# Later weights split into high and low parts by converting and adding GpSimd transfers, with new order lists

## The reference, cut to what matters

```
h0  = concat(cls_tok, patches @ W_tok.T)
x   = bi_wkv(ln(h0) @ Wk.T, ln(h0) @ Wv.T) * sigmoid(ln(h0) @ Wr.T) @ Wo.T   # scans over 37 rows
h1  = ... + sigmoid(xn @ Wr_f.T) * (relu(xn @ Wk_f.T)**2 @ Wv_f.T)            # channel mix
c   = top-4 of sigmoid(h1n @ router.T) within the 2 best of 4 groups, scaled
out = h1 + sum_e c_e * (silu(h1n @ gWg[e].T) * (h1n @ gWu[e].T)) @ gWd[e] + shared expert
```

## Time and profile before

| | |
|---|---|
| median of 3 runs | 259.08 us (258.5 to 260.05) |
| the profiled execution | 259.53 us, span 257.6 us |
| PE busy | 245.2 us, 95% |
| DVE busy | 191.2 us, 74% |
| ACT busy | 151.5 us, 59% |
| POOL busy | 17.1 us, 7% |
| PE clock granted, mean | 0.996 of full speed |

### The profile page before, as it was taken

One profiled execution on the slowest core, in us unless ns is written; L12 is line 12 of the kernel. 1 busy time (PEld: TensorE's weight loads), 2 busy tenths in 40 slices (PEclk: granted clock), 3 DMA queues, 4 the chain that ended last, 5 costly groups with the idle time before them and its releaser, 6 DMA issues.

```text
span 257.6 us, 4492 instructions
## 1 busy us (share of the span) xinstructions
PE 245.2 (95%) x1508; PEld 222.6 (86%) x1508; DVE 191.2 (74%) x491; ACT 151.5 (59%) x312; POOL 17.1 (7%) x26
## 2 busy tenths in 40 slices
PE   6988879999999998999999999999999999999994
PEld 4866458578588898999999999999999999999993
DVE  4459988999989998999797799887333175853542
ACT  2399798988868998853795971426441432132220
POOL 5100202003101000101100000101000010000000
PEclk9999999999999999999999999999999999999998
DMA  5668563000000342000003520000144000015500
GB/s 154 211 191 286 212 186 119 0 3 0 0 0 6 84 111 57 0 3 0 1 3 121 187 76 4 1 3 0 54 163 158 29 3 0 1 23 109 102 29 26
DMA packets 13015, 17.49 MB, mean 68 GB/s; under 512 B 2336, under 2 KB 11074, under 8 KB 12866
## 3 DMA queue, kind: packets, MB, share of 16 engines
q1 hardware_dynamic: 12722, 17.11, 22.3%
q10 hardware_dynamic: 272, 0.11, 0.2%
HBM read 16.22 MB, written 0.99 MB: 67 GB/s over the span
## 4 chain that ended last, share of the span: by engine, by line
PE 74%; DVE 9%; ACT 9%; issue 3%; DMA 2%; POOL 0%; SPq 0%; DVEq 0%; POOLq 0%; ACTq 0%
PE PG L964 18%; PE PA L984 17%; PE PG L966 11%; PE PF L984 7%; PE PQ L964 4%; PE PQ L966 3%; PE PX L1001 2%; PE PF L1001 2%; ACT norm L417 2%; DMA w_tok<-in_w_tok 2%; PE PF L974 1%; PE PG L1119 1%; PE PG L1118 1%; DVE K L763 1%; PE PF L991 1%
## 5 line engine op out<-in xcount | busy, mean ns | idle before, releaser
L575 ACT ACTIVATE act<-PG,columns 128x222 f32<-128x222 f32 (+3 forms) x56 | 28.4, 507 | 59.0 <-PE PG L966 45.9
L964 PE MATMUL PG<-stack,hi_egu 128*128 128x222 f32 (+1 forms) x288 | 62.2, 324 | 0.0
L913 DVE SCALAR_TENSOR_TENSOR hid<-PG,columns,act 128x222 f32<-128x222 f32 (+1 forms) x52 | 27.3, 524 | 29.3 <-PE PG L966 26.7
L984 PE MATMUL PA<-w_ed,hid 128*124 128x192 f32 (+1 forms) x240 | 46.1, 327 | 0.6 <-DVE hid L922 0.5
L964 PEld LDWEIGHTS PG<-stack,hi_egu 128*128 128x128 f32 x288 | 45.7, 191 | 0.9 <-DVE hid L913 0.4
L966 PE MATMUL PG<-stack,lo_egu 128*128 128x222 f32 (+1 forms) x192 | 42.8, 304 | 0.0
L984 PEld LDWEIGHTS PA<-w_ed,hid 128*124 128x124 f32 (+1 forms) x240 | 38.6, 183 | 1.3 <-issue 1.3
L966 PEld LDWEIGHTS PG<-stack,lo_egu 128*128 128x128 f32 x192 | 31.8, 191 | 0.0
L391 POOL TENSOR_TENSOR rstd<-var,minus_half 112x2 f32<-112x2 f32 (+3 forms) x12 | 13.8, 1146 | 191.7 <-DVE var L657 191.7
L922 DVE TENSOR_TENSOR hid<-hid,gates 128x222 f32<-128x222 f32 (+1 forms) x48 | 21.9, 461 | 1.6 <-DMA gates<-c_rows 0.7
L984 PE MATMUL PF<-w_down,mix_hid 128*124 128x192 f32 (+1 forms) x120 | 22.8, 326 | 0.0
(11 more groups left out here) (248 smaller groups left out, 441.3 us busy)
## 6 DMA issues: line engine op xcount, KB each, us to landing
gates<-in_w_egu SPq DMA_DIRECT2D x6, 512.0 KB, 4.9
gates<-c_rows SPq DMA_DIRECT2D x16, 138.8 KB, 2.9
gates<-c_rows SPq DMA_DIRECT2D x16, 92.5 KB, 2.7
gates<-c_rows SPq DMA_DIRECT2D x16, 83.2 KB, 2.5
w_ed<-in_w_ed SPq DMA_DIRECT2D x1, 1152.0 KB, 6.1
gates<-c_rows SPq DMA_DIRECT2D x16, 55.5 KB, 2.5
gates<-in_w_up SPq DMA_DIRECT2D x2, 384.0 KB, 4.5
pat<-in_patches SPq DMA_DIRECT2D x2, 370.0 KB, 4.3
```

The lines of the kernel that those rows point to most:

```text
L575: nc.scalar.activation(act[128 - gate:128, n % 2, 0:G.n], PG[0:gate, gate_bank(n), 0:G.n], ACT.Silu, bias=bias).then_inc(act_silu, 1)
L913: V_.scalar_tensor_tensor(out, PG[part, 1, 0:G.n], bias, act[part, i, 0:G.n], ALU.add, ALU.mult).then_inc(mul_done, 1)
L964: mm(out, w_hi[:, slot, cols], x[:, p, 0:G.n], start=(p == 0), stop=False, skip_group_check=True)
L984: last = mm(tile_out(P, G, t), src[:, G.ts[t]:G.ts[t] + G.tp], w, start=start and t != 1, stop=stop, skip_group_check=True)
```

## The change

`rf`, `up0`, `up1`, `sgu` and `egu0` to `egu5` no longer go through the ring. POOL starts a transfer from DRAM straight into `hi` that converts to fp32r (`W:` steps of POOL). ACT writes minus the high part into `lo` (`L:` steps of ACT), and POOL starts a second transfer of the same weight that adds the fp32 value onto `lo` (`L:` steps of POOL). PE waits for that second transfer. The low-part matmuls of PE, the copies of ACT at L409 and L400 for these weights and the subtractions of DVE for `rf`, `up` and `sgu` are gone. `router` moves ahead in the ring, and SP's list gets shorter. The exponents' subtractions on PE now use PSUM tile PA instead of PQ, PX and PG, with the waits changed to suit. All four order lists are new; POOL's list now has 12 roots and 20 transfers.

```diff
+            def pool_casts(pool):
+                for name, _ in CAST:
+                    nc.gpsimd.dma_start(hi[name][:, :, :], A[f"w_{name}"]).then_inc(cast_in[name], 16)
+                    yield name
+
+            def pool_lows(pool):
+                for n, (name, _) in enumerate(CAST):
+                    pool.wait_ge(act_minus, n + 1)
+                    nc.gpsimd.dma_start(lo[name][:, :, :], A[f"w_{name}"], accum_op=ALU.add).then_inc(low_in[name], 16)
+                    yield name
...
-        def act_low_parts(act_e):
-
-            for i, (name, _, _, cols, _) in enumerate(PIECES[FIRST_EGU:]):
-                for s in range(2):
-                    act_e.wait_ge(pe_low, 2 * i + s + 1)
-                    nc.scalar.activation(lo[name][:, s, :], PA[:, s, 0:cols], ACT.Copy).then_inc(act_low, 1)
-                    yield f"{name}{'ab'[s]}"
+        def act_minus_parts(act_e):
+
+            for name, _ in CAST:
+                act_e.wait_ge(cast_in[name], 16)
+                nc.scalar.activation(lo[name][:, :, :], hi[name][:, :, :].bitcast(F32), ACT.Copy, scale=-1.0).then_inc(act_minus, 1)
+                yield name
...
         def need(pe, name):
-            split(pe, PIECE_AT[name] + 1)
+            if name in low_in:
+                pe.wait_ge(low_in[name], 16)
+            else:
+                pe.wait_ge(lo_done, PIECE_AT[name] + 1)
...
-        def pe_low_parts(pe):
...
         def sub_bank(g, i):
-            return PG[:, :, :].rearrange("p b c -> p (b c)") if g else (PQ, PX)[i % 2]
+            return PA[:, :, :].rearrange("p b c -> p (b c)") if g else PA[:, i % 2, :]
...
-POOL_ORDER = [(1, 0), (1, 1), (2, 0), (1, 2), (3, 0), (2, 1), (1, 3), (3, 1), (2, 2), (3, 2), (2, 3), (3, 3)]
+POOL_ORDER = _order(
+    "R0:root1 R1:root1 W:rf W:up0 W:up1 W:sgu L:rf L:up0 W:egu0 W:egu1 W:egu2 W:egu3 W:egu4 L:up1 L:sgu R0:root2 R2:root1",
+    "W:egu5 R0:root3 L:egu0 L:egu1 L:egu2 R1:root2 L:egu3 L:egu4 L:egu5 R3:root1 R1:root3 R2:root2 R2:root3 R3:root2",
+    "R3:root3",
+)
 PE_ORDER = _order(
...
+    "H:early0 H:early1 H:early2 H:early3 F0:tok0 H:early4 H:early5 H:tok H:stats0 H:stats1 H:aggr F0:tr1a F0:tr1b F1:tok0",
+    "F1:tok1 F0:k F0:kt F0:v F0:rt F0:r H:var H:rstd H:scan0 F0:sub0 F0:sub1 F0:sub2 F1:tr1a F1:tr1b F2:tok0 H:scan1 F1:k",
+    "F1:kt H:sb0 F0:o0 F1:v F1:rt F1:r F2:tok1 H:sb1 H:e1 H:edge M0:tr2 F1:sub0 F1:sub1 F1:sub2 M0:rf M0:up0 M0:up1 M0:mix0",
+    "M0:up2 M0:mix1 M0:up3 F2:tr1a M0:mix2 M0:up4 M0:mix3 F2:tr1b M0:up5 M0:mix4 M0:mix5 F1:o0 F1:o1 M0:tr3 F2:k G0:g0",
+    "M0:logits G0:g1 F2:kt G0:v1 G0:g2 M1:tr2 G0:v2 G0:g3 F2:v D0:cT D0:d1 G0:v3 G0:g4 D0:d0 F2:rt G0:v4 G0:g5 F2:r M1:rf",
...
 ACT_ORDER = _order(
...
+    "W:cls W:mask W:k F0:tok0 W:v W:r F0:ln1 F0:tr1a F0:tr1b Z0:x0 F1:tok0 F1:tok1 F0:k F0:kt F0:vt F0:kf F0:v F0:rt F0:r",
+    "F0:exps F0:expe F1:ln1 W:router F0:w0 F0:w1 F0:w2 F0:wr F1:tr1a F1:tr1b L:rf L:up0 F1:k F1:kt F1:vt F1:kf L:up1 F1:v",
+    "L:sgu L:egu0 F2:tok0 F1:rt F1:r F1:exps F2:tok1 M0:ln2 Z1:x0 F1:expe F1:w0 M0:tr2 F1:w1 F2:ln1 F1:w2 F1:wr M0:rf",
+    "M0:mix0 M0:mix1 M0:mix2 M0:mix3 F2:tr1a M0:mix4 M0:mix5 L:egu1 F2:tr1b L:egu2 L:egu3 M0:ln3 M0:tr3 Y0:e0 F2:k",
...
+    "M1:mix0 F2:expe M1:mix1 F2:w0 F2:w1 F2:w2 F2:wr M1:mix2 Y0:e6 M1:mix3 Z2:x0 F3:tok0 Y0:e7 L:egu5 Y0:e8 M1:mix4 F3:ln1",
...
 DVE_ORDER = _order(
...
+    "W:cls W:mask F0:stats1 F0:aggr1 F0:var1 F0:ln1 W:k W:v W:r F0:tr1a F0:tr1b F1:stats1 F1:aggr1 F0:scan0 F0:scan1",
+    "F1:var1 F0:sb F0:e1 F0:edge F0:top0 F0:top1 F0:sa F1:ln1 F0:ab00 F0:ab01 F0:ab10 F0:ab11 F0:weigh0 F0:weigh1 F0:own",
+    "F0:sum F1:tr1a F0:sum2 F1:tr1b F0:den F0:recip0 F0:recip1 W:router F0:z F1:scan0 F0:x10 F0:x1 F1:scan1 M0:stats2",
+    "M0:aggr2 F1:sb M0:var2 F1:e1 M0:ln2 F1:edge F1:top0 F1:top1 F1:sa F2:stats1 F2:aggr1 F1:ab00 F2:var1 F1:ab01 F1:ab10",
+    "F2:ln1 F1:ab11 M0:tr2a M0:tr2b F1:weigh0 F1:weigh1 F1:own F1:sum F1:sum2 F1:den F1:recip0 F1:recip1 F1:z M0:gated",
+    "M0:h1 M0:stats3 M0:aggr3 M0:var3 F1:x10 M0:ln3 F2:tr1a F2:tr1b F1:x11 F1:x1 M0:tr3a M0:tr3b M1:stats2 M1:aggr2 M1:var2",
```

More of the change, by code:

```diff
@@ L64, in _pieces, with _cast_pieces @@
     yield from ((m, 128, 2, cols, True) for m, cols in (("k", 256), ("v", 128), ("r", 256)))
-    yield ("rf", 128, 2, C, True)
-    yield from ((f"up{i}", 128, 2, HID // 2, True) for i in range(2))
     yield ("router", 128, 2, EXPERTS, True)
-    yield ("sgu", 128, 2, 2 * C, True)
-    yield from ((f"egu{i}", 128, 2, 512, True) for i in range(ECH // 2))
+def _cast_pieces():
+    yield ("rf", C)
+    yield from ((f"up{i}", HID // 2) for i in range(2))
+    yield ("sgu", 2 * C)
+    yield from ((f"egu{i}", 512) for i in range(ECH // 2))
 WHOLE = [("tok", 128, 2), ("o", 128, 2), ("down", 128, UPS), ("sd", 128, SCH), ("ed", 128, ECH)]
@@ L74 @@
 PIECE_AT = {p[0]: n for n, p in enumerate(PIECES)}
+CAST = list(_cast_pieces())
 RING, RING_COLS = 4, 2 * 512
 PERIODS = ECH // 3
-FIRST_EGU = PIECE_AT["egu0"]
 SPANS = ((0, 0, 96, 0), (0, 96, 128, 1), (1, 0, 64, 1), (1, 64, 128, 2), (2, 0, 32, 2), (2, 32, 128, 3))
@@ L106, in at @@
             return g * per_group[s] + n
[L108 to L113, removed]
         def since(engine, s, g):
@@ L121, in build @@
         lo = {p[0]: sb(f"lo_{p[0]}", [p[1], p[2], p[3]], F32R) for p in PIECES if p[4] and p[0] != "router"}
+        for name, cols in CAST:
+            hi[name], lo[name] = (sb(f"{part}_{name}", [128, 2, cols], F32R) for part in ("hi", "lo"))
         router = sb("router", [128, 2, 2 * EXPERTS], F32R)
@@ L233, in build @@
         hi_done, lo_done = sem("hi_done"), sem("lo_done")
-        pe_low, act_low = sem("pe_low"), sem("act_low")
+        cast_in, low_in = ({name: sem(f"{part}_in_{name}") for name, _ in CAST} for part in ("cast", "low"))
+        act_minus = sem("act_minus")
         consts_in = sem("consts_in")
@@ L314, in piece @@
                 if n >= RING:
-                    split(sp, n - RING + 1)
+                    sp.wait_ge(lo_done, n - RING + 1)
                 sp.dma_start(raw[n % RING][0:prt, 0:slots * cols],
@@ L331, in gates_across @@
                 if g == 0:
-                    split(sp, len(PIECES))
+                    sp.wait_ge(lo_done, len(PIECES))
                 for j in range(PERIODS):
@@ L355, in _ @@
             patches(1)
-            for n in range(6, 8):
-                piece(n)
             unsplit("down")
-            for n in range(8, 10):
-                piece(n)
             unsplit("sd")
-            for n in range(10, 13):
-                piece(n)
             unsplit("ed")
-            for n in range(13, len(PIECES)):
-                piece(n)
             patches(2)
@@ L392, in root, with pool_roots @@
                                         minus_half[0:G.tp, 0:cols, 0:G.tiles], ALU.pow).then_inc(pool_rstd[n], 1)
-            for n, g in POOL_ORDER:
-                root(n, g, 2 if n == 1 else 1)
+            def pool_roots(pool, g):
+                for n in (1, 2, 3):
+                    root(n, g, 2 if n == 1 else 1)
+                    yield f"root{n}"
+            def pool_casts(pool):
[7 more added lines that the diff above has]
+                    yield name
+            tracks = tracks_of(pool, pool_casts, R=pool_roots)
+            advance({**tracks, "L": pool_lows(pool)}, POOL_ORDER)
         def act_high_parts(act_e):
@@ L593, in _ @@
             tracks = tracks_of(act_e, act_high_parts, F=act_front, Z=act_first_rows, M=act_mid, Y=act_experts, C=act_gates)
-            advance({**tracks, "L": act_low_parts(act_e)}, ACT_ORDER)
+            advance({**tracks, "L": act_minus_parts(act_e)}, ACT_ORDER)
         V_ = nc.vector
         def dve_low_parts(v):
-            for n, (name, prt, slots, cols, has_lo) in enumerate(PIECES[:FIRST_EGU]):
+            for n, (name, prt, slots, cols, has_lo) in enumerate(PIECES):
                 src = raw[n % RING][0:prt, 0:slots * cols].rearrange("p (s c) -> p s c", s=slots)
@@ L1072, in pe_front @@
                     pe.wait_ge(act_kvr, at(act_kvr, g - 1, 6))
-                elif g == 2:
-                    pe.wait_ge(exp_out, at(exp_out, 0, 4))
                 pe_rows(pe, G, P[bank], a, b, parts, "mask").then_inc(pe_tok, 3 - G.rounds)
@@ L1110, in pe_front @@
                 if g:
-                    pe.wait_ge(act_kvr, at(act_kvr, g, 6))
+                    pe.wait_ge(exp_out, at(exp_out, g - 1, 5))
                 pe.wait_ge(top_ready, g + 1)
@@ L1190, in pe_units @@
             if g == 0:
-                pe.wait_ge(exp_out, at(exp_out, 1, 6))
+                pe.wait_ge(act_kvr, at(act_kvr, 1, 6))
             for n in range(UNITS):
@@ L1217, in pe_downs @@
             else:
-                split(pe, len(PIECES))
+                pe.wait_ge(exp_out, at(exp_out, 1, 5))
             for n in DOWNS:
@@ L1235, in _ @@
         def _(pe):
-            tracks = tracks_of(pe, pe_low_parts, F=pe_front, M=pe_mid, G=pe_units, D=pe_downs)
```

(3 more changed lines are left out.)

## The result

The changed kernel takes 269.12 us (median of 4 runs, 267.67 to 271.31) against 259.12 us for the kernel before on the same chip (258.5 to 260.05): a ratio of 1.039, 95% interval 1.0311 to 1.0469. It is 10.0 us slower, where 3.0 us faster was forecast, and outside the range. The profiled execution took 269.53 us with a span of 267.7 us; that of before 259.53 and 257.6.

A forecast was written before the change was run, and what follows sets the result against it. DVE was taken to bound the kernel up to the first gate product, then nearly fixed PE work. Terms -3.3 (head), -0.5 (ACT), +0.3 (root2), +0.5 (egu0) gave -3.0: 256.1 us against the median 259.08, range 253.8 to 262.3.

The forecast's parts named there:

- nearly fixed work of PE: From first gate product to last down product, 179.3 us before; growth of this stretch was named as a sign of error.
- The head: Stretch up to the first gate product, set by DVE; that product was to start at 71.0 instead of 74.04 us.
- the low halves: Twelve PE steps of 1.09 us before the first gate product, 13.1 us in all; removing them was counted at nothing.
- the term of -3.3: Gain in the head from shorter DVE work and waits: 3.3 us, bounds 2.0 and 4.1.
- the 0.5 us: ACT's gain after the first gate product, where ACT is full, partly from two fewer table loads; between 0 and 1.1.
- POOL's queue: Root2 of group 0 stands behind nine transfer starts, taken at 1.2 us each: 10.8 us, so 0.5 late.
- the term of +0.3: Cost of a late root2 at M0:ln2: 0.5 us late, half of it perhaps made good by ACT's slack.
- L:egu0 for G0:g2: Adding transfer taken to land in 6.9 us, at 74.6 us, 0.5 late for its user due at 74.1.
- the sign named for being wrong: Adding transfers landing over 7 us after issue would show the forecast wrong.
- the later ones have room: Adding transfers after L:egu0 cost nothing, since a unit takes over 3 us and each weight serves two.
- 9.8 us as an upper bound for a landing: High bound for an adding transfer of 512 KB, twice the plain one's 4.9 us; L:egu0 would be 3.4 late.
- the gain is lost in the new lists: Rival: from 74 us on the head start ends in waits elsewhere, or PE's clock falls; about 258.8 us, chance 0.12.

The follow-up runs named there:

- experiment 10: Same kernel as experiment 8, run again for a profile of an ordinary execution and a second interval; 258.08 us, ratio 0.994 against the kernel before.
- both mends: Changed kernel with the edits of experiment 1 and experiment 3 together (output store first, adding transfers early); 258.04 us, ratio 0.9963 against the kernel before.
- experiment 2: Changed kernel without the six adding transfers of egu0 to egu5, PE waiting for ACT's part instead; 264.01 us, ratio 1.0191 against the kernel before.
- experiment 3: Changed kernel with the adding transfers started earlier: egu0 to egu2 at 43 to 55 us, the others at 68 to 70.5; 262.41 us, ratio 1.0129.
- experiment 1: Changed kernel with SP storing group 1's output ahead of group 2's router rows and gates; 263.92 us, ratio 1.0189 against the kernel before.
- experiment 7: Kernel of experiment 1 with the ten transfers of the low parts converting but not adding; 258.67 us, ratio 0.9969 against the kernel before.
- experiment 9: Kernel before, with only SP's two lines exchanged: group 1's store ahead of group 2's router rows and gates; 261.81 us, ratio 1.0115.
- experiment 5: Kernel of experiment 1 with the adding transfer L:egu4 alone put behind Y0:e7; 259.59 us, interval 0.9968 to 1.003 against the kernel before.
- experiment 6: Kernel of experiment 1 with L:egu0 to L:egu2 started early, L:egu3 at 69 us, L:egu4 left amid the broadcasts; 259.37 us, interval 0.9974 to 1.0021.
- experiment 8: Kernel with both mends plus five more idle matmuls ahead of F1:k; 257.21 us, ratio 0.9929 against the kernel before.

## Why the prediction was wrong

**Where the 10 us are.** By the profiled executions: to the first gate product -2.8 us. From there to SP's start of group 0's router rows 8.35 us, as before (8.37). From group 0's to group 1's rows 58.4 us against 52.0: +6.4. From there to the last down product 125.6 against 119.0: +6.6. In experiment 10, with both mends, these two stretches are 52.8 and 119.5 us, so +0.8 and +0.5 of it belongs to the lists, and about 5.6 and 6.1 us to the two holes. The prediction took this whole way, from the first gate product to the last down product, as nearly fixed work of PE (179.3 us); it grew to 192.3 us, which it had named as a sign of being wrong. By the medians the holes are 5.2 and 6.8 us (experiments 2 and 3) and 5.2 us (experiment 1).

**The head: right.** The forecast for the first gate product was 71.0 us, it was 71.21; scan0 of group 0 was to start at 18.8 and started at 17.78 us. The sum over DVE gave this without the low halves, and with the clock at 0.91 or 1.00 the head ended at the same time (71.03 and 71.28 us), so counting them at nothing was right. On this measure 3.0 us were forecast and 2.83 came; whether the other 0.3 us of the term of -3.3 came too is not shown.

**ACT: not seen.** ACT has 6 table loads instead of 8, and those at 102.65 and 104.63 us are gone, as forecast. But the stretch from group 0's to group 1's rows, where the 0.5 us should show, is 0.8 us longer even with both mends.

**POOL's queue: the price too high.** I took 1.2 us for a start. A converting start took 0.54 to 1.02 us, an adding one 0.86 to 1.00, and one of them 1.52. Root2 was not late: POOL stood idle for 0.22 us in front of it until DVE's variance was there (41.48 us). DVE waited 0.61 us for it ("less than 1 us" was forecast), and the kernel before already had 0.52 us there. So the term of +0.3 was about nothing. DVE was busy for 18.47 of 20 us in 20 to 40 us, and the adding starts between 30 and 41 us took 0.87 to 1.00 us; the one of 1.52 us is among the three from 67.99 us on. By the trap that the Trainium skill describes ("SBUF — State Buffer", SBUF: two separate sides) starts would stretch while DVE is in a two-port mode. None but that of 1.52 us could bear the rule out, and no trace shows which mode DVE was in.

**L:egu0 for G0:g2: nothing.** 0.5 us late was forecast. The adding transfers landed 3.7 to 9.2 us after their start, median 6.9 (the value I took; the sign named for being wrong was 7), and PE waited for none of them. By the estimate from the Trainium skill ("DMA: Bandwidth & Descriptors", Anatomy of one DMA) it would have been 3.2 us; the trace does not agree, neither for these nor for the transfers without an add in experiment 7 (median 4.3 us).

**The step that failed** is the sentence under "The adding transfers" that the later ones have room. It asked only whether a low part would be there for its own product. It did not ask what else needs the transfer engines at 68 to 90 us. Group 0's router rows and gates do, and they had about 1 us of room. 9.8 us as an upper bound for a landing held here (9.2 us), but nothing was put on the neighbours: the effect on the write (3.6 instead of 1.4 us) and on the broadcasts (up to 5.6 us) was a term left at nothing without a reason. Experiments 2, 3 and 7 show it: take the adding transfers away, move them, or leave out the add, and 5.2 to 6.8 us come back.

**The second failure** is the rival "the gain is lost in the new lists". It was the right kind of case, but priced as the loss of the gain only (258.8 us) with a chance of 0.12, and no place was named. A walk along SP's program with the new lists would have found one: `D2:cT` and with it group 2's rows come later (53.6 us after group 1's rows, before 47.6), `M3:gated` does not (ready 70.4 us after them, before 71.3), and the store is queued between them behind 13 us of broadcasts. That is 5.2 us, shown by experiment 1; experiment 9 shows that it is the pairing of list and SP order.

**The lists themselves** cost about 1.3 us: three waits of PE for ACT at 112.90, 130.43 and 134.46 us (0.68, 0.28 and 0.30 us), where the kernel before had none between 101 and 140 us. All three stand ahead of group 1's rows and are there in experiment 10 too (0.66, 0.29 and 0.30 us), so they can account for the 0.8 us above and not for the 0.5; this was not tried by itself.

**The clock** makes the holes dearer than their waits: behind each PE was granted the lower level (0.50), from 93 to past 95 us and from 215.7 to 219 us. Behind a wait of 4.37 us the clock of 90 to 100 us was 0.83, behind 4.99 us (experiment 1) 0.68; behind waits of about 1 us (experiments 5 and 6) it was 1.00. The text named the head as the place for a low clock. There it fell too (0.91 over 20 to 40 us), and cost nothing that experiments 8 and 10 can tell.

## What to carry to other kernels

When transfers are moved, ask who else's small transfer is in flight then, and how much slack it has. The profile before doesn't print the room of a wait that isn't there; it has to be added up along the chain (write, starts, landing) against the time at which the user is ready. Here that was about 1 us for group 0, while the only wait for a gate before (0.75 us at 235.01 us) was group 3's and said nothing about it. When order lists change, walk the queue of every engine that has none of them (here SP) against the new order: a store that was never waited for can stand behind 13 us of something else. Judge an order of such a queue only together with the lists: the same exchange brought 5.2 us in one kernel and cost 3.0 in the other.

## What the runs showed of the hardware

- Adding transfers of GpSimd held the transfer engines for longer per byte than converting ones at the same places: share 0.55 against 0.33 over the same 20 us at about 100 GB/s, landing in 6.9 against 4.3 us (median), and 0.89 against 0.54 us of POOL to start one (experiments 1 and 7).
- The time to landing is not a property of the kind alone: in the changed kernel the six converting transfers of 512 KB into `hi`, five of them started between 32 and 36 us among adding ones, took 8.0 us (median).
- A write of 13.9 KB behind four adding transfers took 3.2 to 5.1 us instead of 1.4 us, though the last was started 5 us before; behind four converting ones it took 2.0 us.
- Behind 4.4 us without a matmul PE was granted half of the full clock (0.50 in 93 to 95 us of the changed kernel); behind 0.95 us it kept 1.00 (88.7 to 90.2 us of experiment 5).
- One execution of the kernel of experiment 8 took 1315 us: all matmuls were several times as long (eight of 128x192 in 8.37 us instead of 1.5), though the records give a granted clock of 1.00. It isn't in the median of 257.21 us; why it happened is open.
